# A decoder layer on one core: cross-attention and expert products in one block, with splits, routing and normalisation reordered

## What is computed

```
def _layernorm(x, axis=-1, eps=1e-05): ...
x = x + _L0_attn_ref(_layernorm(x, axis=-1), L0_attn_w_qkv, L0_attn_w_out)      # causal, 16 heads of 32
x = x + _L0_xattn_ref(_layernorm(x, axis=-1), mask_BxSx4224_bf0, ctx_2048, ctx_2048,
                      L0_xattn_wq, L0_xattn_wk, L0_xattn_wv, L0_xattn_wo)        # one head of 512
x = x + _L0_ffn_ref(_layernorm(x, axis=-1), L0_ffn_wg, L0_ffn_W, L0_ffn_b)
```

## Time and profile before

| what | value |
|---|---|
| median of three launches | 758.77 us |
| the profiled launch | 760.28 us |
| its span (first to last instruction) | 758.4 us |
| TensorE busy | 682.1 us |
| VectorE, ScalarE, GpSimd busy | 501.7, 309.4, 330.4 us |
| first block (self-attention) | to 342.6 us |
| second block (cross-attention) | 342.6 to 664.4 us |
| third block (expert products) | 664.4 to 758.4 us |

### The profile page before, as it was taken

How to read it: one execution, slowest core, us unless ns; L and a number is a source line. 1 busy time by engine, 2 the same in 40 slices (tenths; PEclk the granted TensorE clock), 3 DMA queues, 4 the chain that set the end, 5 groups by cost and what they waited for, 6 DMA issues and landing times. The chain is left out here.

```text
span 758.4 us, 19014 instructions
## 1 busy us (share of the span) xinstructions
PE 682.1 (90%) x6040; PEld 606.2 (80%) x6041; DVE 501.7 (66%) x1478; ACT 309.4 (41%) x985; POOL 330.4 (44%) x558
## 2 busy tenths in 40 slices
PE   4768999999999999999999999999999986379995
PEld 4757898989888878878899999999999965257884
DVE  4767788888787878846555555556564559464663
ACT  3445565666655666623132323232323263012220
POOL 4376757575766786714101010101010155654652
PEclk9879999999999999999999999999999998579998
DMA  6477875655656657719914233343420245366530
GB/s 249 147 153 136 118 145 116 149 133 126 141 123 135 139 112 137 180 43 309 328 38 113 54 113 53 111 55 111 55 105 6 73 121 193 85 103 217 177 103 13
DMA packets 142744, 95.09 MB, mean 125 GB/s; under 512 B 110702, under 2 KB 114926, under 8 KB 142576
## 3 DMA queue, kind: packets, MB, share of 16 engines
q1 hardware_dynamic: 137040, 82.00, 45.3%
q0 software_dynamic: 5664, 12.61, 6.1%
HBM read 56.14 MB, written 18.77 MB: 99 GB/s over the span
## 5 line engine op out<-in xcount | busy, mean ns | idle before, releaser
L508 ACT ACTIVATE prob<-prob,shift 128x128 f32<-128x128 f32 (+1 forms) x256 | 114.5, 449 | 116.6 <-POOL shift L419 116.1
L1302 ACT CAST w_hi<-b_bank 128x256 fp32r<-128x256 f32 (+1 forms) x132 | 56.4, 445 | 161.0 <-PE b_bank L60 139.6
L60 PE MATMUL b_bank<-w_hi 128*128 128x256 f32 (+1 forms) x536 | 110.5, 329 | 5.7 <-DVE w_lo L1472 5.7
L60 PE MATMUL a_job<-w_hi 128*128 128x256 f32 (+1 forms) x488 | 94.5, 317 | 16.0 <-DVE w_lo L711 7.6
L60 PE MATMUL b_bank<-w_lo,w_hi 128*128 128x256 f32 (+1 forms) x536 | 107.0, 322 | 0.0
L60 PE MATMUL b_bank<-w_hi,w_lo 128*128 128x256 f32 (+1 forms) x536 | 106.2, 320 | 0.0
L732 DVE CUSTOM_DVE_ANT_0 prob<-a_s,mask 128x128 f32<-128x128 f32 (+1 forms) x256 | 79.6, 347 | 30.1 <-PE a_s L608 29.9
L1472 DVE TENSOR_TENSOR w_lo<-b_bank,w_hi 128x256 fp32r<-128x256 f32 (+1 forms) x132 | 63.0, 507 | 50.8 <-ACT w_hi L1302 50.3
L60 PEld LDWEIGHTS b_bank<-w_hi 128*128 128x128 f32 x536 | 82.9, 193 | 12.6 <-DVE w_lo L1472 3.7
L60 PEld LDWEIGHTS a_job<-w_hi 128*128 128x128 f32 x488 | 71.3, 195 | 25.8 <-DVE w_lo L711 8.2
L60 PEld LDWEIGHTS b_bank<-w_lo,w_hi 128*128 128x128 f32 x536 | 84.1, 192 | 7.9
(11 more groups left out here) (173 smaller groups left out, 1149.7 us busy)
## 6 DMA issues: line engine op xcount, KB each, us to landing
stage<-in_w SPq DMA_DIRECT2D x6, 1024.0 KB, 8.4
xin<-in_x SPq DMA_DIRECT2D x8, 512.0 KB, 4.2
xr<-in_x SPq DMA_DIRECT2D x8, 512.0 KB, 3.9
x<-xr SPq DMA_DIRECT2D x8, 512.0 KB, 3.2
xin<-x SPq DMA_DIRECT2D x8, 512.0 KB, 9.6
xr<-x SPq DMA_DIRECT2D x8, 512.0 KB, 4.4
x2n<-x_sb SPq DMA_DIRECT2D x8, 512.0 KB
x2n<-xn_sb SPq DMA_DIRECT2D x8, 512.0 KB, 6.9
```

The source lines that it names most:

```text
L60: ins = pe_matmul(out, a, b, start=first and i == 0, stop=last and i == len(steps) - 1)
L508: a = nc.scalar.activation(prob[:, e % NPROB, cols], prob[:, e % NPROB, cols], ACT.Exp, scale=-1.0, bias=shift[:, e, q:q + 1], accum_out=r ...
L1302: nc.scalar.copy(hi, src).then_inc(job_hi, 1)
```

## The change

1. `mixture_of_experts` becomes a class `Products`, whose methods are called at the end of each engine's part of `cross_attention`. The block's end and barrier between them are gone. Its PSUM banks are the first four of cross-attention's ring, and its output rows lie in `xin` and `xn`.
2. The context's two tiles lie in `stage[2]`; the experts' buffers and the order of their high parts change. Experts 0, 1 and 2 get their high parts inside batch 6 (after q3, k3 and v1), 4 and 3 after p1 of batch 7, 5 and 7 after o3, 6 after y1.
3. GpSimd: expert 0's low part before the rsqrt of batch 6; expert 1's and 2's earlier; `store_entries` of batch 6 before the low parts of 4 and 3 instead of behind those of 2 and 4. It no longer splits 5 and 6: VectorE does, with 7.
4. The last batch on VectorE is written out (`last_batch`): batch 6 is chosen before its scores, `place_tokens` and `known_blocks` come before the o jobs' low parts, each of the two tiles of rows is normalised by itself, and batch 7 is chosen and placed here. The order is s0 s1 p0 p1 o0 o1 o2 o3 y0 y1 Y0 l0 Y1 l1; p works by query tile.
5. SyncE: the loads of 5, 7 and 6 and then the 7 table reads and the bias load come before the stores of batch 7's rows. Gathers 0 to 4 are bounded to the rows of batches 0 to 6; gather 5 is the first that waits for all stores.

```diff
-    BUFFER = (0, 1, 2, 3, 4, 0, 1, 2)
+    BUFFER = (0, 1, 4, 3, 2, 0, 2, 1)
+
+    HIGH_ORDER = (0, 1, 2, 4, 3, 5, 7, 6)
...
+        flat = stage[CONTEXTS][:].rearrange("p c n -> p (c n)")
+        cin = flat[:, 0:TB * D].rearrange("p (t n) -> p t n", t=TB)
+        cin_t = flat[:, TB * D:].rearrange("p (c n) -> p c n", c=DC)
+        assert TB * D + DC * S == DC * D
...
-        LAST = [j for j in ORDER if j[0] not in FRONT]
+        LAST = "s0 s1 p0 p1 o0 o1 o2 o3 y0 y1 Y0 l0 Y1 l1".split()
...
-            for e in (0, 1, 2, 4):
+            for e in (0, 1, 2):
...
+            sp.wait_ge(ct_split, B - 1)
+            sp.wait_ge(c_split, B - 1)
+            experts.load(sp, w, 4)
             batch(B - 2, True, False)
-            batch(B - 1, False, False)
+            for e in (5, 7, 6):
+                experts.load(sp, w, e)
             sp.wait_ge(blocks.known_done, 2)
             sp.wait_ge(routing.entries_in, 16 * TB * (B - 1))
             for k in range(Blocks.KNOWN):
                 blocks.entries(sp, routing.table, 0, k)
+            for e in (2, 3):
+                experts.wait_split(sp, e)
+            sp.dma_start(bias_sb[:], bass.AP(tensor=bias.tensor, offset=bias.offset, ap=[[0, P], [1, E * D]]))\
+                .then_inc(bias_in, 16)
+            batch(B - 1, False, False)
+            products.sync(sp)
 
         @block.gpsimd
...
+            experts.low(nc.gpsimd, 0)
             rstd_ln3(B - 2)
             routing.store_entries(nc, pool, tick_pool, B - 3)
             experts.low(nc.gpsimd, 1)
             routing.next_tokens(nc, pool, tick_pool, B - 3)
-            for e in (2, 4):
+            experts.low(nc.gpsimd, 2)
+            routing.store_entries(nc, pool, tick_pool, B - 2)
+            for e in (4, 3):
                 experts.low(nc.gpsimd, e)
-            routing.store_entries(nc, pool, tick_pool, B - 2)
-            experts.low(nc.gpsimd, 5, (0, 1))
-            rstd_ln3(B - 1)
-            experts.low(nc.gpsimd, 5, (2, 3))
-            experts.low(nc.gpsimd, 6)
             routing.next_tokens(nc, pool, tick_pool, B - 2)
             for stored in x2n_out:
                 pool.wait_ge(stored, 16 * (B - 1))
-            for k in (0, 1):
-                blocks.first_gather(nc, pool, tick_pool, experts, k)
+
+            def rstd_tile(t):
+                pool.wait_ge(ln3_dve, (B - 1) * 5 + 3 * (t + 1))
+                nc.gpsimd.tensor_tensor(rstd[:, 1, t:t + 1], veps[:, 1, t:t + 1], expo[:, t:t + 1], ALU.pow)\
+                    .then_inc(ln3_rstd, 1)
+
+            blocks.first_gather(nc, pool, tick_pool, experts, 0)
+            rstd_tile(0)
+            blocks.first_gather(nc, pool, tick_pool, experts, 1)
+            rstd_tile(1)
+            products.pool(pool)
...
+        FREE = {("q3", B - 2): (0,), ("k3", B - 2): (1,), ("v1", B - 2): (2,), ("p1", B - 1): (4, 3), ("o3", B - 1): (5, 7)}
...
+                    for e in FREE.get((j, n), ()) if isinstance(n, int) else ():
                         experts.high(nc, act, e)
-                    if j == route_after(n) and has_routing(n):
+                    if j == route_after(n) and order(n) is ORDER and has_routing(n):
                         routing.exponentials(nc, act, n - 1)
...
-            with act.Fori(1, B - 1) as n:
+            with act.Fori(1, B - 2) as n:
                 batch(n)
-
-            act.wait_ge(job_done, done_at("v1", B - 2))
-            for e in range(STAGED):
-                experts.high(nc, act, e)
+            batch(B - 2)
+            routing.exponentials(nc, act, B - 2)
             batch(B - 1)
             act.wait_ge(job_done, done_at("y1", B - 1))
-            for e in (6, 7):
-                experts.high(nc, act, e)
+            experts.high(nc, act, 6)
+            products.act(act)
 
...
-                    if j == ("o3" if order(n) is ORDER else "o1") and has_routing(n):
+                    if j == ("o3" if order(n) is ORDER else "s1") and has_routing(n):
                         routing.count(nc, pe, n - 1)
 
             batch(0)
             with pe.Fori(1, B - 1) as n:
                 batch(n)
             batch(B - 1)
-
...
+            def tile_stats(t, n):
+                first = n * 5 + 3 * t
+                dve.wait_ge(job_ev, ev_at(f"y{t}", n))
+                dve.sem_inc(tick, 1)
+                nc.vector.bn_stats(stats[:, 1, t, :], x2_sb[:, t, :]).then_inc(ln3_dve, 1)
+                dve.wait_ge(ln3_dve, first + 1)
+                dve.sem_inc(tick, 1)
+                nc.vector.bn_aggr(mv[:, 1, t, :], stats[:, 1, t, :]).then_inc(ln3_dve, 1)
+                dve.wait_ge(ln3_dve, first + 2)
+                nc.vector.tensor_scalar(veps[:, 1, t:t + 1], mv[:, 1, t, 1:2], EPS, None, ALU.add).then_inc(ln3_dve, 1)
+
+            def tile_apply(t, n):
+                if t == 0:
+                    wait(dve, xn3_out, 16 * n)
+                dve.wait_ge(ln3_rstd, n + 1 + t)
+                nc.vector.tensor_scalar(xn3_sb[:, t, :], x2_sb[:, t, :], mv[:, 1, t, 0:1], rstd[:, 1, t:t + 1],
+                                        ALU.subtract, ALU.mult).then_inc(xn3_ready, 1)
+
+            def last_batch(n):
+
+                dve.wait_ge(job_ev, ev_at("l1", n - 1))
+                dve.sem_inc(tick, 1)
+                routing.choose(nc, dve, n - 1)
+                scores_max("s0", n)
+                scores_max("s1", n)
+                routing.gates(nc, dve, n - 1)
+                lo_part("p0", n)
+                lo_part("p1", n)
+                routing.place_tokens(nc, dve, n - 1)
+                nc.vector.reciprocal(rinv[:], rsum[:]).then_inc(rinv_done, 1)
+                blocks.known_blocks(nc, dve, routing)
+                for j in ("o0", "o1", "o2", "o3"):
+                    lo_part(j, n)
+                experts.low(nc.vector, 5)
+                add_output("y0", n)
+                tile_stats(0, n)
+                experts.low(nc.vector, 7, (0, 1))
+                tile_apply(0, n)
+                add_output("y1", n)
+                tile_stats(1, n)
+                move_rows("Y0", n)
+                tile_apply(1, n)
+                experts.low(nc.vector, 7, (2,))
+                move_logits("l0", n)
+                move_rows("Y1", n)
+                experts.low(nc.vector, 7, (3,))
+                experts.low(nc.vector, 6, (0,))
+                move_logits("l1", n)
+                dve.wait_ge(job_ev, ev_at("l1", n))
+                dve.sem_inc(tick, 1)
+                routing.choose(nc, dve, n)
+                experts.low(nc.vector, 6, (1, 2, 3))
+                routing.gates(nc, dve, n)
+                routing.place_tokens(nc, dve, n)
 
             batch(0)
             dve.wait_ge(routing.consts, Routing.CONSTS)
             with dve.Fori(1, B - 2) as n:
                 batch(n)
             batch(B - 2)
-            experts.low(nc.vector, 0)
-            batch(B - 1)
...
+class Products:
...
+            batches = B - 1 if isinstance(i, int) else B
+            if k == self.FIRST:
+                for stored in x2n_out:
+                    pool.wait_ge(stored, 16 * B)
+            pool.wait_ge(gather_no_done, m + 1 - AHEAD)
+            blocks.gather(pool, tick_pool, k, batches)
...
+        def step(i, k):
+            transposes(i, k)
+            if isinstance(i, int) and k == 0:
+                routing.count(nc, pe, B - 1)
+            if isinstance(i, int) and k == 1:
+                experts.all_split(pe)
+            if k >= 1:
+                product(i, k - 1)
```

450 lines of the change are left out of this document (229 added, 221 removed).

## The result

| what | before | after |
|---|---|---|
| median of six launches each, on one chip | 760.15 us (758.11 to 762.05) | 755.33 us (752.68 to 756.65) |
| the profiled launch | 760.28 us | 756.65 us |
| its span | 758.4 us | 754.9 us |

The ratio is 0.9935, with a 95% interval of 0.9912 to 0.9959. The kernel became faster, as forecast, but by 4.8 us where 14.8 were predicted (the two profiled launches lie 3.6 us apart, their spans 3.5; the profiled launch after is the slowest of its six). 755.33 lies outside the range of 739.5 to 751.0.

A forecast was written before the change was run, and what follows sets the result against it. TensorE's arithmetic, busy 90% of the span, bounds the kernel; only its idle time can be won. 9.4 + 3.4 + 1.1 + 0.9 = 14.8 us off the median of 758.77 gives 744.0 us, range 739.5 to 751.0.

The forecast's parts named there:

- Part 1: Logits' end to product 0: without the barrier 5.5 us instead of 14.9, a gain of 9.4 us.
- the cover of 3 us: Before product 0: gather 0 would be in at about 646, ahead of the transposes at about 649.
- Part 2: y1's end to the logits' end: 9.9 us instead of 13.3, a gain of 3.4 us, bounds 0 and 6.
- Part 3: Start of the y pair: y0 at 632.0 instead of 633.15, a gain of 1.1 us, bounds 2.2 and -3.
- The remaining four or five dependent operations may each wait for a piece: `known_blocks` on VectorE: each operation may wait for one GpSimd split operation, so it ends between 627 and 632.
- one GpSimd piece: VectorE's operations with two SBUF inputs stretch by about one GpSimd split operation: 0.68 to 1.42 us, and one of 3.11.
- Rival 2: GpSimd's splits of 4 and 3 hold `known_blocks` and expert 5 on VectorE: 9 to 11 us won, 748 to 750, chance 0.22.
- Part 4: Stall at block 4: gather 4 issued about 2.1 us after product 0 instead of 3.0, a gain of 0.9 us.
- It still takes 10.9 us: Gather 4 at block 4: its own time stays at 10.9 us, so the stall shrinks by 0.9 us.
- The 5.9 us: Gathers before product 0: gather 1 had landed at most 5.9 us after its issue, so gather 0 comes before the transposes.

The follow-up runs named there:

- the wait: The kernel after, with GpSimd waiting for `known_blocks` before its splits of experts 4 and 3: ratio 0.9852 to the kernel before, 746.34 us.
- memset and wait: The kernel after, with a tiny GpSimd `memset` and a wait for its end before the split of expert 4: ratio 0.9861 to the kernel before.
- `known_blocks` late: The kernel after, with `known_blocks` on VectorE moved behind the low parts of o0 to o3: ratio 0.9916 to the kernel before.
- the longer run: The kernel before, with GpSimd's four pieces of expert 5's split in one run ahead of the power: 757.45 us in one launch, 1.000.
- the power first: The kernel after, GpSimd waiting for `known_blocks` before its splits and computing each tile's power before issuing its gather: ratio 0.9879 to the kernel before.
- the rows first: The kernel after, GpSimd waiting for `known_blocks`, y rows' residual and statistics before VectorE's expert splits, both powers before `next_tokens` and gathers: ratio 0.9882 to the kernel before.
- the biases late and the power first: The kernel after, GpSimd waiting for `known_blocks`, powers before gathers, bias load behind the stores of batch 7's rows: ratio 0.9805 to the kernel before, 749.65 us.

## Why the prediction was wrong

**Part 1, the seam: right.** 5.5 us expected from the logits' end to product 0, 5.0 measured; a gain of 9.9 instead of 9.4. Expert 6's three pieces took 1.88 us together for the 2.0 assumed. No gather held product 0: gather 0 was issued at 645.25 and gather 1 at 650.44, where I had both issued by 642.9, but everything else was late too. Gather 1 took 8.8 us and was in 0.6 us before its transposes (659.93), so that no gather held product 0 was close, and the cover of 3 us was not there.

**Part 2, y1 to the logits: right.** 9.9 expected, 9.45 measured: a gain of 3.85 instead of 3.4.

**Part 3, y0's start: wrong, and nearly all of the miss.** It was to come 1.1 us earlier and came 8.5 later, far beyond my bound of -3. At y1's end the loss was 8.4 us, so the term is 9.5 us off. The step that failed is the sentence "The remaining four or five dependent operations may each wait for a piece", and its "ends between 627 and 632". It was one operation that waited, for all eight pieces. The step rests on reading the 3.11 us of the earlier trace rows as "one GpSimd piece": the row lasted from 636.50 to GpSimd's idle, two pieces and more. Had I put VectorE's and GpSimd's rows side by side, I would have seen that both ended together, and that the splits of the earlier trace rows at 626.20, which take turns at 1.42 us, do not stand behind an indirect DMA.

The Trainium skill (SBUF — State Buffer, section SBUF: two separate sides) has the lock between the two engines, and says that the loser waits out one whole instruction. After an idle moment that is what the traces show (1.13 to 1.30 us for each small operation). Behind indirect DMAs without one, they show 3.1 to 10.4 us, a run of two, four or eight instructions. So where the prediction says that the rows agree, that holds for its pieces of 1.42 us and not for the 3.11. Here the measurement decides.

**Rival 2** named the mechanism, GpSimd's splits holding `known_blocks`, and gave 748 to 750 with a chance of 0.22. It had the same price per piece and so y0 at 634 to 636 for 641.62. The experiments that give GpSimd its idle moment ahead of both splits have y0 at 630.9 (the wait) and 634.2 (memset and wait): this is what rival 2 and the forecast were about. With the wait 11.4 of the 14.8 us are won.

**Part 4, block 4: wrong by 1.4 us.** I took 0.9 as the gain, since the gather was to be issued earlier against product 0; it was issued 2.7 us after it instead of 3.0, but took 11.71 us instead of 10.92, and the wait grew from 1.99 to 2.56. -0.5 lies within the bounds of 3.8 and -2. The step that was off is "It still takes 10.9 us": the gather's own time, which lay between 6.2 and 11.7 us in these kernels, moves the wait as much as its issue does. With `known_blocks` late it was issued the same 2.7 us after product 0, took 9.4, and was not waited for.

**A term that I did not have:** the prediction says "So the end moves with the start of product 0, plus what changes at block 4", and so puts what follows the last scatter at no change. GpSimd's drain at the end of the last block takes 5.14 us after the change (5.137 in each of its versions) and 3.82 before (3.823, also with the longer run), 1.3 us more. Why is open. So the sum reads 9.9 + 3.85 - 8.4 - 0.5 - 1.3 = 3.55 us for a span 3.5 us shorter.

**Gathers.** The 5.9 us that I took from the earlier trace rows held for the quiet stretch before the barrier. Beside the biases' load gather 1 took 9 to 12 us, and 5.7 with that load behind it. In four experiments TensorE waited for gather 0 or 1 ahead of product 0: 1.98 us with memset and wait, 2.79 with the power first, 5.64 with the rows first, 5.97 with the biases late and the power first.

## What to carry to other kernels

When GpSimd goes straight from indirect DMAs into a run of SBUF operations, look at what VectorE does with SBUF inputs meanwhile. A small operation that ends just when GpSimd's run ends has probably been shut out by it, and all that stands behind it in VectorE's queue has waited too. One semaphore wait that makes GpSimd idle for a tenth of a microsecond gave back 6 us here. And price such a row by laying both engines' rows side by side, not by the nearest multiple; a stall read as "one piece" grows with the run that it really waits for.

## What the hardware showed that I had not expected

- Behind indirect DMAs VectorE was shut out for as long as GpSimd's run lasted: 3.11 us for two pieces, 5.44 and 5.55 for four, 10.34 and 10.44 for eight, 7.13 for the rest of eight. After 0.09 to 1.25 us of idle on GpSimd such runs let it in after each piece.
- An operation with one input in PSUM (o3's low part) took 0.42 us inside such a run.
- Small `TENSOR_SCALAR` operations, with one tensor in SBUF, wait like the two-input ones: 1.13 to 1.30 us instead of 0.17 to 0.23.
- The gather of block 4, issued 1.3 us behind the second indirect DMA of `store_entries`, took 9.4 us in one kernel and 11.7 in another, and 6.2 when issued 4.1 us behind it. With 9.4 us the clock granted around block 4 was 1.00, with 11.7 it was 0.83.
- GpSimd's drain at the end of the last block took 3.82 us in both kernels with three blocks of code and 5.14 in all eleven with two, begun when the last scatter had landed. At the old barrier it took 6.06 us, and ended 0.7 us after gather 1 had landed.
